# Local attention in six layers on one Trainium2 core: norms in the scores' PSUM banks, and an order of work of its own for each of four tiles

## Chip, cores and metric

One core of a Trainium2 chip runs the whole program, launched once. The metric is the time on the device in microseconds (us). The kernel before took 3695.43 us, the median of three runs (3693.75 to 3704.42).

## What is computed

For a batch of 8, 512 tokens of 128 features: a layer norm with modulation, a plain causal attention (16 heads of 8), a second modulation, and then six layers, each a windowed attention and a feed-forward. The change is in the six layers alone:

```python
def attn_layer(x, Wqkv, qs, ksc, Wo):
    q, k, v = jnp.split(x @ Wqkv, 3, -1)          # 16 heads of 64
    q, k = l2norm(q) * qs, l2norm(k) * ksc        # a norm for each token and head
    q = q * cos * scale + rotate_half(q) * sin * scale
    k = k * cos / scale + rotate_half(k) * sin / scale
    out = local_attention(q, k, v)                # windows of 32; keys of this window and the one before
    return out @ Wo
def ffn_layer(x, g, bln, W1, b1, W2, b2):
    xn = (x - mu) / jnp.sqrt(var + 1e-05) * g + bln
    a, gate = jnp.split(xn @ W1 + b1, 2, -1)
    return a * jax.nn.gelu(gate) @ W2 + b2
for i in range(6):
    x = attn_layer(shift_tokens(x), ...) + x
    x = ffn_layer(shift_tokens(x), ...) + x
```

## The kernel before

`program` calls three parts; `part_a` is the first attention, `part_c` the output, and `part_b` the six layers. `part_b` goes through NSEQ = 48 pairs of layer and batch element ("sequences"), each in TILES = 4 tiles of 128 tokens: NT = 192 tiles. All code is unrolled; each engine has its own list, written by a Python loop over steps g (`for g in STEPS`, on POOL over t), and one step does the same for every tile. What belongs to a whole sequence (output projection, mean, variance, feed-forward) is hung into the steps by `seq_at(g, lag)`, which is true in one step of four.

For a tile k the chain is: `project(c, k)` on PE multiplies x with the weights for q (c = 0) and k (c = 1), each product in three f32r passes (lines 919 to 921), into the PSUM banks `proj`. ACT squares them (`squares_of`, L1177). DVE multiplies with the two rotary tables (`turns_of`, L1385 and L1391) and sums the squares by head (`square_sums`, L1399); POOL adds the halves (`add_halves`, L1325). `norms_of` (from L1403) makes the inverse roots of the 32 sums of a tile with nine small instructions on DVE, each waiting for the one before: a clamp (L1411), a first guess from the bit pattern (L1420, with the constant table `magic`), four for a cubic step and three for a Newton step (L146 to L162). All their operands are in SBUF. In one step of four the variance of the feed-forward's norm goes along. POOL scales the heads (`scale_heads`, L1331). PE transposes (`transpose_qk(k, i)`, i = 0 to 3, L958), ACT empties into qT and kT (`qk_out`).

Scores: ACT writes the window's mask into the two PSUM banks `scr` (L1251), `score(k, half)` adds 64 matmuls of 32 queries by 64 keys on quarters of the array (L979), DVE takes the maximum (L1458) and subtracts it (L1460), ACT does exp (L1232), DVE sums and inverts (L1470, L1473), POOL scales (`L1345`). PE transposes the probabilities (`transpose_probs`, L992), and `weigh(k, half)` does 128 matmuls on quarters of the array (L1013), whose values SP has copied into place with seven DMAs per tile (L885); SP waits for the weigh of the tile before. `output` (L1028), `mean` (L1036), `variance` (L1041), `spread` (L1049), `feed_up` (L1055) and `feed_down` (L1064) follow by sequence.

PSUM is full: four banks `proj`, two `scr`, two `ring`. The ring's two banks take in turn every transpose, the values and the weighed values, ten fills a tile; `ring_order` gives the order, and PE, ACT and SP count by it.

The order of PE in one step g is: T3(g-1), score(g-1, 0), values(g-1, 0), transpose_probs(g-2, 0), score(g-1, 1), transpose_probs(g-2, 1), values(g-1, 1), project(0, g+1), weigh(g-2) in both halves, project(1, g+1), T0, T1, T2 of g, with the work by sequence in between. So score 0, score 1 and weigh are three blocks apart from one another in every step.

## Time and profile before

| | us |
|---|---|
| median of three runs | 3695.43 |
| lowest, highest | 3693.75, 3704.42 |
| profiled execution, its span | 3699.1 |
| PE busy | 3521.4 |
| DVE busy | 3039.5 |
| ACT busy | 2586.6 |
| POOL busy | 2309.1 |

TensorE's operations in the timeline from 1500 to 1565 us, from the first start to the next operation's, where nothing stalls:

| operation | us |
|---|---|
| project (6 matmuls) | 1.50 |
| values (3) | 0.79 |
| four transposes | 0.44 |
| a score half (64) | 0.79 |
| weigh, both halves (128) | 2.00 |
| feed_up (2 passes) | 0.86 |
| output (16) | 3.46 |
| feed_down (6) | 2.58 |

The six layers take from about 630 us to 3680 us. A busy PE is not PE at its peak: the ends of matmuls are modelled and overlap. "Issue" in a list of waits is idle time that no semaphore explains. PE is TensorE's matmuls, PEld its weight loads; both come from one stream of instructions.

### The profile page before, as it was taken

The page shows a single profiled execution, that of the slowest core. Times are in us where ns is not written, and L with a number is a line of the kernel's source. Part 1 is how long each engine was busy: PE and PEld are TensorE (multiplying, and loading weights), DVE is VectorE, ACT ScalarE, POOL GpSimd, SP SyncE. Part 2 cuts the span into 40 slices and gives each one's busy share as a digit, 9 for nine tenths or more (in the row PEclk, how much of TensorE's full clock was granted, in tenths as well). Part 3 has the DMA queues.
Part 4 walks back from the last instruction along what each step waited for, and adds up shares of the span by engine and source line. Part 5 has one row for each costly group of instructions (what it writes and reads, how often), then busy time and mean ns, then how long its engine had stood idle before and what let it go on. Part 6 is the DMA issues. An engine that isn't in the chain of part 4 may idle for free. (4 is left out here: it accounts for less than half of the span.)

```text
span 3699.1 us, 146879 instructions
## 1 busy us (share of the span) xinstructions
PE 3521.4 (95%) x63940; PEld 2694.0 (73%) x63940; DVE 3039.5 (82%) x4947; ACT 2586.6 (70%) x4028; POOL 2309.1 (62%) x1364
## 2 busy tenths in 40 slices
PE   6999996999999999999999999999999999999996
PEld 4777774777777777777777777777777777777774
DVE  5767766988889988888888888888898888888883
ACT  3565554677777777777777777777777777777773
POOL 1110104767777777777777767777777777776761
PEclk9999998999999999999999999999999999999998
DMA  2000001212222222222222222222222222222212
GB/s 75 4 4 7 4 7 43 56 48 58 56 58 63 64 56 58 56 56 62 58 56 58 54 56 64 56 58 55 64 63 58 56 57 54 56 56 54 54 49 68
DMA packets 121989, 188.76 MB, mean 51 GB/s; under 512 B 24942, under 2 KB 43142, under 8 KB 120972
## 3 DMA queue, kind: packets, MB, share of 16 engines
q1 hardware_dynamic: 121356, 179.36, 18.7%
q8 instruction: 514, 8.42, 1.0%
q14 instruction: 119, 0.97, 0.1%
HBM read 24.08 MB, written 4.19 MB: 8 GB/s over the span
## 5 line engine op out<-in xcount | busy, mean ns | idle before, releaser
L1325 POOL TENSOR_TENSOR rc<-rc,rs 128x1024 f32<-128x1024 f32 x384 | 912.9, 2377 | 349.2 <-DVE rs L1391 348.5
L1331 POOL TENSOR_TENSOR rc<-rc,rnorm 128x1024 f32<-128x1024 f32 x384 | 723.7, 1906 | 392.9 <-DVE rnorm L162 331.4
L1385 DVE TENSOR_TENSOR rc<-proj,rope_b 128x1024 f32<-128x1024 f32 x384 | 466.7, 1215 | 96.1 <-ACT squares L1177 89.6
L1177 ACT ACTIVATE squares<-proj 128x1024 f32<-128x1024 f32 x384 | 394.0, 1026 | 151.1 <-PE proj L921 137.6
L1013 PEld LDWEIGHTS ring<-pT,vmoved 64*64 64x64 f32 x18432 | 381.2, 135 | 132.8 <-issue 132.8
L1391 DVE TENSOR_TENSOR rs<-proj,rope_b 128x1024 f32<-128x1024 f32 x384 | 466.2, 1214 | 0.0
L958 PEld LDWEIGHTS ring<-ident,rc 128*128 128x128 f32 x3072 | 364.2, 142 | 137.5 <-issue 52.2
L1399 DVE TENSOR_REDUCE sums<-squares 128x16 f32<-128x1024 f32 x384 | 455.3, 1186 | 1.1 <-issue 0.9
L1013 PE MATMUL ring<-pT,vmoved 64*64 64x32 f32 x18432 | 407.7, 220 | 37.9 <-issue 36.4
L958 PE MATMUL ring<-ident,rc 128*128 128x128 f32 x3072 | 426.3, 277 | 11.6 <-POOL rc L1331 6.6
L1013 PE MATMUL ring<-pT,vown 64*64 64x32 f32 x6144 | 381.9, 219 | 13.8 <-issue 13.8
L1345 POOL TENSOR_TENSOR prob_b<-prob_b,rinv 128x1024 f32<-128x1024 f32 x192 | 366.4, 1909 | 12.5 <-DVE rinv L1473 12.5
L979 PEld LDWEIGHTS scr<-kT,qT 64*32 64x32 f32 x24576 | 270.3, 105 | 134.0 <-issue 133.1
L919 PE MATMUL proj<-wqkv_hi,xa_hi 128*128 128x512 f32 x768 | 344.7, 449 | 18.2 <-POOL xa_lo L1307 12.1
L979 PE MATMUL scr<-kT,qT 64*32 64x64 f32 x24576 | 338.5, 224 | 15.6 <-issue 15.2
L1028 PE MATMUL proj<-oT_b,wo 128*128 128x256 f32 x1536 | 347.6, 379 | 1.3 <-issue 1.3
L1013 PEld LDWEIGHTS ring<-pT,vown 64*64 64x64 f32 x6144 | 334.7, 135 | 12.7 <-issue 12.7
L744 DVE TENSOR_REDUCE negmax<-tm 128x1 f32<-128x384 f32 (+3 forms) x352 | 220.6, 639 | 144.5 <-PE tm L420 141.0
L586 ACT ACTIVATE probT<-km 128x512 f32<-128x512 f32 (+1 forms) x352 | 193.3, 559 | 204.9 <-PE km L436 196.6
L1168 ACT ACTIVATE kT<-ring 128x512 f32<-128x512 f32 x384 | 231.1, 602 | 139.9 <-PE ring L958 139.7
L1168 ACT ACTIVATE vown<-ring 128x512 f32<-128x512 f32 x384 | 229.0, 596 | 122.3 <-PE ring L921 111.7
L1028 PEld LDWEIGHTS proj<-oT_b,wo 128*128 128x128 f32 x1536 | 284.4, 190 | 36.2 <-issue 1.4
(176 smaller groups left out, 7886.1 us busy)
## 6 DMA issues: line engine op xcount, KB each, us to landing
vmoved<-vown SPq DMA_DIRECT2D x576, 128.0 KB
vmoved<-vown SPq DMA_DIRECT2D x192, 192.0 KB
vmoved<-vown SPq DMA_DIRECT2D x576, 64.0 KB
wqkv_raw<-in_L_ffn_Wqkv SPq DMA_DIRECT2D x40, 192.0 KB, 2.7
wo<-in_L_ffn_Wo SPq DMA_DIRECT2D x6, 512.0 KB, 4.2
x_attended<-xtok SPq DMA_DIRECT2D x8, 256.0 KB, 2.0
xtok_c<-x_attended SPq DMA_DIRECT2D x8, 256.0 KB, 4.2
out<-xtok_c SPq DMA_DIRECT2D x8, 256.0 KB, 2.4
```

Of the source, the lines that this page charges most:

```text
L958: last = nc.tensor.transpose(bank[:, p * P:(p + 1) * P], rc[:, k % 2, c, o:o + P], ident[:, :])
L979: last = nc.tensor.matmul(scr[32 * w:32 * w + 32, s, p, :], qT[rows, p, 32 * w:32 * w + 32], kT[rows, p, j * P + 32 * w:j * P + 32 * w + K ...
L1013: last[i] = nc.tensor.matmul(banks[i][64 * b:64 * b + 64, p, 32 * odd:32 * odd + 32], v[64 * s:64 * s + 64, :], pT[64 * s:64 * s + 64, p, ...
L1028: last = nc.tensor.matmul(bank[:, HALVES[half]], wo[:, p, :], oT[:, p, HALVES[half]], start=(p == 0), stop=(p == PAIRS - 1))
L1168: nc.scalar.activation(dst, src, ACT.Copy).then_inc(ring_free, 1)
L1177: nc.scalar.activation(squares[:, c, :], proj[c][:, :], ACT.Square).then_inc(sq_done, 1)
L1325: nc.gpsimd.tensor_tensor(rc[:, k % 2, c, :], rc[:, k % 2, c, :], rs[:, c, :], ALU.add).then_inc(add_done, 1)
L1331: nc.gpsimd.tensor_tensor(dst, dst, rnorm[:, k % 2, c * HEADS:(c + 1) * HEADS].rearrange("p (h o) -> p h o", o=1).broadcast_to([P, HEADS, ...
L1345: nc.gpsimd.tensor_tensor(pr, pr, rinv[:, :, :].rearrange("p q (s o) -> p q s o", o=1).broadcast_to([P, PAIRS, 2, KEYS]), ALU.mult).then_i ...
L1385: nc.vector.tensor_tensor(rc[:, k % 2, c, :].rearrange("p (h d) -> p h d", h=HEADS), proj[c][:, :].rearrange("p (h d) -> p h d", h=HEADS), ...
L1391: nc.vector.tensor_tensor(rs[:, c, :].rearrange("p (h s d) -> p h s d", h=HEADS, s=2), src[:, :, ::-1, :], tab.broadcast_to([P, HEADS, 2, ...
L1399: nc.vector.tensor_reduce(sums[:, c * HEADS:(c + 1) * HEADS], squares[:, c, :].rearrange("p (h d) -> p h d", h=HEADS), AX.X, ALU.add).then ...
```

## The change

The loops over steps go. `ring_order` and each engine's list are now written for a round of four tiles, `for n in ROUNDS`, every operation with its own tile (4n + something), in an order that differs from tile to tile. Semaphores that counted q and k together are split in two (`proj_full`, `sq_done`, `ss_done`, `turned_done`, `add_done`, `unit_done`), since q and k no longer come in a fixed turn; waits that the order gave for nothing are written out (`after`, `turned`, and some in ACT's and DVE's functions). SP's list is unchanged.

The norms use the first of the two `scr` banks (`powers`) for the sums and the running term between the subtraction of one tile's maxima and the masks of another: `norms_of(k)` waits until tile k - 2 is subtracted, and `mask_scores(k)` until the norms of tile k + 1 are done. The steps are rearranged so that no instruction has two operands in SBUF; they become ten (`cubic_powers` has five). `magic` and its memset go.

ACT and POOL now split the first chunk of the second layer's weights before their first round. In the diff, whole orders stand for PE and DVE, a stretch of ACT's; those of ACT and POOL are rewritten in the same way, with the same operations as before.

```diff
 
-LAST_STEP = NT + 6
+
+NORMS_LEAD = (1, 1, 1, 1)
+SCORES_BACK = (1, 1, 1, 1)
...
-    for g in range(-1, LAST_STEP + 1):
-        mine = [("T3", g - 1), ("V0", g - 1), ("P0", g - 2), ("P1", g - 2), ("V1", g - 1), ("O0", g - 2), ("O1", g - 2),
-                ("T0", g), ("T1", g), ("T2", g)]
+    for n in ROUNDS:
+        mine = [("T3", 4 * n + 2), ("T0", 4 * n + 2), ("T2", 4 * n + 2), ("V0", 4 * n + 2), ("P0", 4 * n + 1),
...
+def cubic_powers(nc, dve, x, y, t, w, sem, base):
+
+    ALU = mybir.AluOpType
+    dve.wait_ge(sem, base + 1)
+    nc.vector.scalar_tensor_tensor(t, x, CUBIC, y, ALU.mult, ALU.mult).then_inc(sem, 1)
+    dve.wait_ge(sem, base + 2)
+    nc.vector.tensor_tensor(t, t, y, ALU.mult).then_inc(sem, 1)
+    dve.wait_ge(sem, base + 3)
+    nc.vector.tensor_tensor(w, t, y, ALU.mult).then_inc(sem, 1)
+    dve.wait_ge(sem, base + 4)
+    nc.vector.scalar_tensor_tensor(t, t, -1.25 / CUBIC, w, ALU.add, ALU.mult).then_inc(sem, 1)
+    dve.wait_ge(sem, base + 5)
+    nc.vector.scalar_tensor_tensor(y, y, 1.875, t, ALU.mult, ALU.add).then_inc(sem, 1)
+
+
...
-        magic = sb("magic", [P, 2 * HEADS + TILES])
...
+        powers = scr[:, 0, :, :].rearrange("p q k -> p (q k)")
...
+        def norms_end(eng, k):
+            eng.wait_ge(rn_done, (min(k + NORMS_LEAD[k % TILES], NT - 1) + 1) * POWER_STEPS)
...
             def score(k, half):
...
-                pe.wait_ge(ring_free, RING[f"T{2 * half + 1}", k] + 1)
-                if half == 0:
-                    need(pe, scr_masked, k)
+                if half == 0 and k == 0:
+                    norms_end(pe, k)
+                    mask_first_scores()
+                pe.wait_ge(ring_free, max(RING[f"T{2 * half}", k], RING[f"T{2 * half + 1}", k]) + 1)
+                need(pe, scr_masked, k)
                 pe.sem_inc(pe_passed, 1)
...
+            for n in ROUNDS:
+                transpose_qk(4 * n + 2, 3)
+                project(1, 4 * n + 4)
+                after(centred, 1, n - 1, 1)
+                after(ffn_read, 1, n - 2, 1)
+                turned(0, 4 * n + 3)
+                variance(n - 1)
+                transpose_qk(4 * n + 2, 0)
+                transpose_qk(4 * n + 2, 2)
+                values(4 * n + 2, 0)
+                transpose_probs(4 * n + 1, 0)
+                after(var_read, 1, n - 1, 1)
+                after(centred, 1, n - 1, 1)
+                after(ffn_read, 1, n - 2, 1)
+                project(0, 4 * n + 4)
+                values(4 * n + 2, 1)
+                transpose_probs(4 * n + 1, 1)
+                score(4 * n + 2, 0)
+                score(4 * n + 2, 1)
+                weigh(4 * n + 1)
+                project(1, 4 * n + 5)
+                transpose_qk(4 * n + 3, 2)
+                transpose_qk(4 * n + 3, 3)
+                turned(0, 4 * n + 4)
+                spread(n - 1)
+                transpose_qk(4 * n + 3, 1)
+                turned(0, 4 * n + 4)
+                output(n, 0)
+                transpose_qk(4 * n + 3, 0)
+                values(4 * n + 3, 0)
+                after(normed, 1, n - 1, 1)
+                after(attn_added, 2, n, 1)
+                project(0, 4 * n + 5)
+                transpose_qk(4 * n + 4, 3)
+                transpose_probs(4 * n + 2, 0)
+                score(4 * n + 3, 0)
+                values(4 * n + 3, 1)
+                transpose_qk(4 * n + 4, 1)
+                score(4 * n + 3, 1)
+                transpose_qk(4 * n + 4, 0)
+                turned(0, 4 * n + 5)
+                feed_up(n - 1, 0)
+                transpose_probs(4 * n + 2, 1)
+                turned(0, 4 * n + 5)
+                feed_up(n - 1, 3)
+                weigh(4 * n + 2)
+                turned(1, 4 * n + 5)
+                feed_up(n - 1, 1)
+                turned(1, 4 * n + 5)
+                feed_up(n - 1, 4)
+                transpose_qk(4 * n + 4, 2)
+                after(gated, 3, n - 1, 1)
+                after(gelu_done, 3, n - 1, 1)
+                project(0, 4 * n + 6)
+                values(4 * n + 4, 0)
+                after(gated, 3, n - 1, 2)
+                turned(1, 4 * n + 5)
+                feed_up(n - 1, 2)
+                score(4 * n + 4, 0)
+                score(4 * n + 4, 1)
+                transpose_probs(4 * n + 3, 0)
+                transpose_probs(4 * n + 3, 1)
+                after(gelu_done, 3, n - 1, 3)
+                after(gated, 3, n - 1, 2)
+                after(gelu_done, 3, n - 1, 2)
+                project(1, 4 * n + 6)
+                weigh(4 * n + 3)
+                turned(0, 4 * n + 6)
+                feed_up(n - 1, 5)
+                values(4 * n + 4, 1)
+                transpose_qk(4 * n + 5, 0)
+                turned(0, 4 * n + 6)
+                output(n, 1)
+                transpose_qk(4 * n + 5, 1)
+                transpose_qk(4 * n + 5, 2)
+                after(attn_added, 2, n, 2)
+                after(gated, 3, n - 1, 3)
+                project(0, 4 * n + 7)
+                values(4 * n + 5, 0)
+                transpose_qk(4 * n + 5, 3)
+                project(1, 4 * n + 7)
+                values(4 * n + 5, 1)
+                transpose_probs(4 * n + 4, 0)
+                score(4 * n + 5, 0)
+                score(4 * n + 5, 1)
+                transpose_probs(4 * n + 4, 1)
+                turned(0, 4 * n + 7)
+                feed_down(n - 1)
+                weigh(4 * n + 4)
+                after(ffn_read, 1, n - 1, 1)
+                turned(0, 4 * n + 7)
+                mean(n)
+                transpose_qk(4 * n + 6, 1)
...
+            def mask_scores(k):
+                if k == 0 or not tile(k):
+                    return
+                act.wait_ge(sub_done, k)
+                norms_end(act, k)
+                mask = win_mask[k % TILES].rearrange("p (s q k) -> p s q k", s=1, q=1)
+                nc.scalar.activation(scr[:, :, :, :], mask.broadcast_to([P, 2, PAIRS, KEYS]), ACT.Copy).then_inc(scr_masked, 1)
...
+            act.wait_ge(raw_in, 16)
+            act.wait_ge(w_lo_done, BATCH)
+            split_hi(BATCH, w_raw[:, :])
...
+                exponentials(4 * n - 1)
+                gelu(n - 2, 0)
+                attention_out(4 * n - 2, 0)
+                gelu(n - 2, 1)
+                attention_out(4 * n - 2, 1)
+                qk_out(4 * n, 2)
+                mask_scores(4 * n)
+                squares_of(0, 4 * n + 2)
+                gelu(n - 2, 2)
+                values_out(4 * n, 0)
...
+            def norms_of(k):
...
+                x, t, y = powers[:, lo:hi], powers[:, 64 + lo:64 + hi], rnorm[:, k % 2, lo:hi]
                 if tile(k):
-                    dve.wait_ge(ss_done, 2 * k + 2)
-                    ss = sums[:, 0:2 * HEADS]
-                    nc.vector.scalar_tensor_tensor(ss, ss, 1e-24, ss, ALU.max, ALU.max).then_inc(clamp_done, 1)
+                    for c in range(2):
+                        dve.wait_ge(ss_done[c], k + 1)
+                        need(dve, unit_done[c], k - 1)
+                    need(dve, sub_done, k - SCORES_BACK[k % TILES])
+                    nc.vector.tensor_scalar(powers[:, 0:2 * HEADS], sums[:, :], 1e-24, None, ALU.max).then_inc(clamp_done, 1)
                 if m is not None:
                     dve.wait_ge(var_full, m + 1)
-                    nc.vector.tensor_scalar(sums[:, 2 * HEADS:], proj_bank(0, 0)[:, 0:TILES], 1e-5, None, ALU.add).then_inc(var_read, 1)
+                    need(dve, spread_done, m)
+                    if not tile(k):
+                        dve.wait_ge(sub_done, NT)
+                    nc.vector.tensor_scalar(powers[:, 2 * HEADS:hi], proj_bank(0, 0)[:, 0:TILES], 1e-5, None, ALU.add).then_inc(var_read, 1)
                     dve.wait_ge(var_read, m + 1)
                 if tile(k):
                     dve.wait_ge(clamp_done, k + 1)
-                    need(dve, unit_done, 2 * k - 2)
-                x, y, t = sums[:, lo:hi], rnorm[:, k % 2, lo:hi], rtmp[:, lo:hi]
-                nc.vector.scalar_tensor_tensor(y.bitcast(i32), x.bitcast(i32), -0.5, magic[:, lo:hi], ALU.mult, ALU.add).then_inc(rn_done, 1)
-                cubic(nc, dve, x, y, t, rn_done, i * RSQRT_STEPS)
-                newton(nc, dve, x, y, t, rn_done, i * RSQRT_STEPS)
-                dve.wait_ge(rn_done, (i + 1) * RSQRT_STEPS)
+                nc.vector.tensor_scalar(y.bitcast(i32), x.bitcast(i32), -0.5, float(0x5F3759DF), ALU.mult, ALU.add).then_inc(rn_done, 1)
+                cubic_powers(nc, dve, x, y, t, rtmp[:, lo:hi], rn_done, i * POWER_STEPS)
+                newton_powers(nc, dve, x, y, t, rn_done, i * POWER_STEPS)
...
+            for n in ROUNDS:
+                less_maxima(4 * n)
+                turns_of(1, 4 * n + 2)
+                add_attention(n - 1, 1)
+                sums_of(4 * n)
+                norms_of(4 * n + 2)
+                square_sums(0, 4 * n + 3)
+                turns_of(0, 4 * n + 3)
+                maxima(4 * n + 1)
+                less_maxima(4 * n + 1)
+                turns_of(1, 4 * n + 3)
+                sums_of(4 * n + 1)
+                centre(n - 1)
+                square_sums(1, 4 * n + 3)
+                norms_of(4 * n + 3)
+                square_sums(1, 4 * n + 4)
+                turns_of(1, 4 * n + 4)
+                turns_of(0, 4 * n + 4)
+                maxima(4 * n + 2)
+                square_sums(0, 4 * n + 4)
+                less_maxima(4 * n + 2)
+                norms_of(4 * n + 4)
+                sums_of(4 * n + 2)
+                apply_deviation(n - 1)
+                add_attention(n, 0)
+                turns_of(1, 4 * n + 5)
+                square_sums(1, 4 * n + 5)
+                turns_of(0, 4 * n + 5)
+                maxima(4 * n + 3)
+                less_maxima(4 * n + 3)
+                square_sums(0, 4 * n + 5)
+                norms_of(4 * n + 5)
+                gate(n - 1, 0)
+                gate(n - 1, 1)
+                sums_of(4 * n + 3)
+                turns_of(0, 4 * n + 6)
+                square_sums(0, 4 * n + 6)
+                maxima(4 * n + 4)
+                square_sums(1, 4 * n + 6)
+                gate(n - 1, 2)
```

## Rows read from the trace of the kernel before

**Rows 1.** The page, part 1: busy us, share of the span, instructions.
```profile
PE 3521.4 (95%) x63940; PEld 2694.0 (73%) x63940; DVE 3039.5 (82%) x4947; ACT 2586.6 (70%) x4028; POOL 2309.1 (62%) x1364
```

**Rows 2.** Busy time by window: stretch, length, busy us (instructions) per engine, granted clock, DMA.
```profile
700.00:3650.00 2950.00, 2871.74 (x58686) 2228.01 (x58684) 2551.45 (x3899) 2196.84 (x3347) 2158.23 (x1232) 1.00 0.23 57
```

**Rows 3.** Waits of PE, 700 to 3650 us: us in total, times, longest us.
```profile
PE ring L1013 <- issue: 48.5, 52, 1.8
PE scr L979 <- issue: 13.6, 30, 1.0
...
PE proj L919 <- DVE rs L1391: 1.5, 1, 1.5
```

**Rows 4.** Line 1036 (mean), its matmuls: duration ns, first and last start.
```profile
L1036 PE MATMUL proj<-xs,mean_w x96: 592/594/668, 709.7 to 3654.1; 128*128 128x512 f32 x96
```

**Rows 5.** The page, part 3: the instruction queue's packets, MB, share.
```profile
q8 instruction: 514, 8.42, 1.0%
```

**Rows 6.** Busy time by window, as rows 2, between the ends of PE's issue stalls.
```profile
1501.10:1533.31 32.21, 30.80 (x626) 24.19 (x625) 27.50 (x43) 22.80 (x36) 24.27 (x14) 1.00 0.23 58
...
1564.34:1590.88 26.54, 26.27 (x500) 20.34 (x500) 22.03 (x34) 18.89 (x31) 20.15 (x12) 1.00 0.27 69
1590.88:1596.80 5.92, 4.74 (x126) 3.86 (x125) 4.55 (x9) 3.91 (x5) 4.58 (x6) 1.00 0.01 3
```

**Rows 7.** DMA queues from 1530.5 to 1530.9 us, then PE's timeline around one stall.
```profile
q8 instruction: 1, 0.02, 17.4%
...
1531.93 0.22 PE L1013 MATMUL ring<-pT,vmoved 64*64 64x32 f32 x1
...
1533.32 0.26 PE L1013 MATMUL ring<-pT,vmoved 64*64 64x32 f32 x4 [1.18 <-issue]
```

**Rows 8.** Timeline of PE: start, us, what, merged count.
```profile
1510.68 0.60 PE L992 MATMUL ring<-ident,prob_b 128*128 128x128 f32 x4
1511.21 0.86 PE L979 MATMUL scr<-kT,qT 64*32 64x64 f32 x64
1512.00 0.66 PE L992 MATMUL ring<-ident,prob_b 128*128 128x128 f32 x4
...
1525.23 0.60 PE L992 MATMUL ring<-ident,prob_b 128*128 128x128 f32 x4
1525.66 0.95 PE L1041 MATMUL proj<-mean_w,hid 128*128 128x1 f32 x8
```

**Rows 9.** Groups of DVE, 700 to 3650 us: line, operation, count, busy, mean ns, idle before.
```profile
L1458 DVE TENSOR_REDUCE rmax<-scr 128x16 f32<-128x1024 f32 x187 | 229.0, 1224 | 25.4 <-PE scr L979 19.8
L1470 DVE TENSOR_REDUCE rsum<-prob_b 128x16 f32<-128x1024 f32 x187 | 226.0, 1208 | 2.2 <-ACT prob_b L1232 2.2
L1438 DVE SCALAR_TENSOR_TENSOR hid<-proj,vec,hid 128x512 f32<-128x512 f32 x141 | 105.7, 750 | 127.9 <-PE proj L1055 107.9 <-ACT hid L1208 20.1
L1411 DVE SCALAR_TENSOR_TENSOR sums<-sums 128x32 f32<-128x32 f32 x185 | 70.9, 383 | 3.2
L1473 DVE RECIPROCAL rinv<-rsum 128x16 f32<-128x16 f32 x187 | 47.3, 253 | 6.5
L150 DVE SCALAR_TENSOR_TENSOR rtmp<-rtmp 128x32 f32<-128x32 f32 (+1 forms) x185 | 35.7, 193 | 6.3
```

**Rows 10.** Groups of ACT and POOL, 700 to 3650 us, as rows 9.
```profile
L1168 ACT ACTIVATE oT_b<-ring 128x512 f32<-128x512 f32 x376 | 202.9, 590 | 41.8 <-PE ring L1013 41.3
L1232 ACT ACTIVATE prob_b<-prob_b 128x1024 f32<-128x1024 f32 x187 | 198.1, 1059 | 25.7 <-DVE prob_b L1460 22.8
L1208 ACT ACTIVATE hid<-proj,vec 128x512 f32<-128x512 f32 x141 | 96.5, 685 | 0.6
L1208 ACT ACT_TABLE_LOAD x47 | 60.3, 1283 | 0.8
...
L1345 POOL TENSOR_TENSOR prob_b<-prob_b,rinv 128x1024 f32<-128x1024 f32 x187 | 356.9, 1909 | 12.5 <-DVE rinv L1473 12.5
```

**Rows 11.** Timeline of SP: a tile's seven moves, issued.
```profile
1533.83 5.43 SPq L885 DMA_DIRECT2D vmoved<-vown  x7
```

628 lines of the change are left out of this document (334 added, 294 removed).

## The prediction

> **What bounds the kernel now.** I read first the page's busy shares: PE is busy for 95% of the span, DVE for 82%, ACT and POOL for less [rows 1]. Then the layers alone, by a window of 2950 us: PE 2871.74 of 2950, DVE 2551.45 (86%), at a granted clock of 1.00 [rows 2]. So TensorE sets the pace, and the question is what its remaining idle time is. The list of waits answers it: of all that PE waits for in that window, 48.5 us (52 times) and 13.6 us (30 times) are put down to "issue", which is no semaphore, and they lie in two lines, L1013 (weigh) and L979 (score). The longest wait of PE for another engine comes to 1.5 us in all [rows 3]. No engine keeps TensorE waiting: an order that only removes waits has nothing to remove here.
>
> One sequence of one layer (four tiles) I call a round. The matmuls of `mean`, one pair a round, start from 709.7 to 3654.1 us, 48 pairs [rows 4]: (3654.1 - 709.7) / 47 = 62.6 us per round, and 2950 / 62.6 = 47 rounds lie in the window.
>
> What are the issue stalls? The instruction queue q8 brought 514 packets, 8.42 MB, so 16.4 KB each [rows 5]; PE and PEld have 63940 instructions each [rows 1], and 127880 / 514 = 249 of them come with a packet. Between the end of one stall and that of another, the windows hold 626 + 625 = 1251, 500 + 500 = 1000 and 126 + 125 = 251 recorded matmuls and weight loads [rows 6]: 5, 4 and 1 times 250. Every stall thus sits on the edge of a packet. One seen closely: the packet is on the queue within 1530.5 to 1530.9, the last matmul before the gap starts at 1531.93, the next at 1533.32, some 2.5 us behind the packet [rows 7]. TensorE has run out of instructions; it had passed the rest of what it held faster than the next 16 KB came. The shown idle time starts at the modelled end of a matmul (0.22 us), so a stall is 0.2 us longer than listed: 62.1 + 82 x 0.2 = 78.5 us, over 47 rounds 1.7 us a round.
>
> Which edges stall? A weigh is 128 matmuls and 128 loads, 256 instructions in some 1.85 us (2.00 with leaving), so each holds about one edge (256 / 251). Of 47 x 4 = 188 weighs only 52 stall, 28%. The tiny matmuls are the only code that eats 16 KB in less than the 2.5 us; an edge in the first part of a weigh was ordered while longer matmuls ran. I read it so: an edge stalls if about the last 0.72 x 256 = 185 instructions before it were all of such a burst. A stall costs (48.5 + 52 x 0.2) / 52 = 1.1 us on average.
>
> **The change, part by part.** What a row-tiled block costs beside its matmuls (seams). The four transposes of L992 take 1525.66 - 1525.23 = 0.43 ahead of `variance` and 1511.21 - 1510.68 = 0.53 ahead of a score: entering costs 0.10. In a score the last of 64 matmuls starts 0.86 - 0.22 = 0.64 behind the first, and the next operation 1512.00 - 1511.21 = 0.79: leaving costs 0.15 [rows 8]. Together 0.25. Before, a tile has three such blocks (score 0, score 1, weigh), 12 a round. In the new PE order tile 4n+2 has score 0, score 1 and weigh(4n+1) in direct succession, 4n+4 and 4n+5 their two score halves together, 4n+3 all three apart: 1 + 2 + 2 + 3 = 8 blocks. Four seams go: 4 x 0.25 = 1.0 us a round, x 48 = **-48 us**. All of it is on the path, PE being dense. The matmuls themselves stay as they are, so nothing else on PE gets shorter.
>
> The supply of instructions, by the same measure. Score, score, weigh in one is a burst of 128 + 128 + 256 = 512. Edges behind its first 185: (512 - 185) / 251 = 1.3 a round. I take 1.4 us each, more than the 1.1 above, since scores pass their 128 instructions in 0.64 us, and 185 of them give the packet less cover: 1.8 us. A double score (256): (256 - 185) / 251 = 0.28 stalls of 1.6 us, 0.45, and 0.1 for edges in the few instructions right behind; two of these, 1.1. The other three weighs 0.28 x 1.1 = 0.3 each, 0.9. The single score halves of tile 4n+3 as now, 0.1 (13.6 + 6 = 20 us / 188 tiles). Together 3.9 us a round against 1.7: +2.2, x 48 = **+106 us**. Bounds: from nothing (the burst is fed after all) to 1.3 x 2.0 (the longest seen, 1.8 + 0.2 [rows 3]) + 2 x 0.7 + 1.0 = 5.0, that is +3.3, +158 us. I take 2.2 because it uses the mean share that stalls now.
>
> Waits. Before there are next to none on PE. In the new order several chains end near where TensorE needs them; the tightest that I find is from score(4n+3) to transpose_probs(4n+3, 0), worked out under the rivals, with 0.6 us left before any hand-off. A few such places, and stalls that shift one engine against another, I take at 0.4 us a round, **+19 us**; bounds 0 and 2 us a round (0 and +96). A wait of PE gives a packet time to land, and both won't be paid where they meet: -10 us.
>
> The norms. Nine small instructions per tile become ten. Most take 193 ns, the first 383 [rows 9]. No row has DVE write PSUM; the nearest small ones are 193 ns and, with 16 columns and another operation, 253 [rows 9]: ten of them are 1.9 to 2.5 us against about 2.0 now, between -0.1 and +0.5 us a tile. DVE has 14% idle, 8.5 us a round; covered, nothing. What it costs is an order: the operands lie in `scr`, so norms(k+1) stands between less_maxima(k-1) and mask_scores(k), on which score(k) waits. That loop (less_maxima, norms, masks as long as an exp, two score halves, maxima, and a turn of DVE besides) is 1.22 + 2.2 + 1.0 + 1.6 + 1.22 + 1.22 = 8.5 us of some 15.7 per tile, and it doesn't set the pace by itself. The memset of `magic` on POOL goes, before anything is measured by it.
>
> At the start ACT now waits for the first chunk of the next layer's weights before its first round (a transfer and a split, before there was anything to hide it): **+4 us**, once; the tail keeps its chain. The DMAs and their bytes stay. SP's seven moves of a tile's values still wait for the weigh of the tile before, and the next weigh for them: issuing them takes 5.43 us [rows 11], landing the last about 1 more. The shortest way in the new order is from weigh(4n+2) to weigh(4n+3), with two feed_up, transposes, project, values, feed_up, two scores, two transposes and project between; by the table of TensorE's operations ahead of the prediction (seams off where halves join) 0.86 x 2 + 0.44 + 1.5 + 0.8 + 0.86 + 1.4 + 0.87 + 1.5 = 9.1 us. 2.6 us are left; covered, nothing.
>
> Sum: -48 + 106 + 19 - 10 + 4 = +71 us. The profiled execution has a span of 3699.1, 3.7 over the median of 3695.4 and inside the spread of the runs; put on the median, 3695.4 + 71 = **3766 us**.
>
> **The rivals.** (a) The supply doesn't get worse, and the seams are saved: -48 + 4 + 0 to 19, 3651 to 3670 us, faster. For it: the share of edges that stall is inferred, not seen, and none of the bursts before is longer than 256. A lead that grows in the slow parts might carry over. Against it: a weigh alone uses up what is held, in 28 of 100 cases. The Trainium skill (Runtime: NRT & Kernel Launch, Instruction fetch mechanics) says that instructions are refilled in blocks of 16 KiB, 256 instructions, and that crossing such a block is mostly hidden, since dispatch is slower than the refill; by that rule this rival is right. The block agrees with the trace (16.4 KB, 251 recorded), the hiding doesn't: 82 stalls in 47 rounds.
>
> (b) The waits decide, on the other side: the chain for the probabilities of tile 4n+3. From the end of its scores DVE does maxima and less_maxima, 2 x 1.22; ACT exp (1.06), a table load of 1.28, gelu 0, one `attention_out` and gelu 1 (0.69 + 0.59 + 0.69), which DVE's gate 1 (0.75) needs, and behind that gate stand sums_of (1.21 + 0.25) and POOL's scale_probs (1.91): 2.4 + 4.3 + 0.75 + 1.46 + 1.91 = 10.9 us, counted from 0 [rows 9, 10]. TensorE has in that stretch T0, feed_up 0, P1, feed_up 3, weigh, feed_up 1 and 4, T2, project, values, feed_up 2 and two scores: 0.44 + 0.86 + 0.44 + 0.86 + 2.0 + 1.7 + 0.44 + 1.5 + 0.8 + 0.9 + 1.6 = 11.5 us by the same table. 0.6 us are left; some eight hand-offs eat it. From there each us is a us a round. Two such places one us late each, beside the supply stalls: +96, 3862 us.
>
> (c) Supply and seams cancel (+1.0 a round instead of +2.2): within 10 us of 3695. This is also what comes out if the new order does nothing for PE, which was never waiting.
>
> **How the numbers follow.** Forecast, 0.55: 3766, its own range 3715 to 3815. (a) 0.20, (b) 0.15, (c) 0.10. Beyond 0.3% (11 us), about what a measurement of this kernel tells from no change: faster 0.22 ((a) and 0.02 of (c)), same 0.10 (0.06 of (c), 0.04 at the lower edge of the forecast), slower 0.68 (0.51, (b), and 0.02 of (c)). The range for 8 in 10 reaches into (a) and (b): 3650 to 3860.
>
> **What would show it.** Right: the round between two `mean` 63.5 to 64.5 us; PE's waits for "issue" about twice as long, most in the weigh behind the two score halves, at multiples of 250 instructions; blocks entered 8 times a round; POOL's and DVE's waits no shorter. Seams: PE busy time per round falls by about 1 us. Wrong: issue stalls at 1.7 us a round or less and a round near 61.5 (rival a); or waits of PE's transposes of the probabilities for POOL, of its scores for ACT's masks, over 1 us a round (rival b). The prediction falls if the stalls don't grow with the length of a burst.

## The result, and the profile after

The changed kernel takes 3876.75 us (median; 3873.32 to 3878.99), the kernel before 3694.65 beside it (3693.75 to 3704.42): a ratio of 1.0496, 95% interval 1.0476 to 1.0516. It is 182 us slower. The prediction, 3766 us, had the direction but only 71 of these 182 us, and the time lies 17 us above its range. Every run's time is the median of executions within 1% of each other; one execution of e7 further down, at 8090.3 us where its other three took 3778.11 to 3795.49, is unexplained and left out.

The page after (parts 1 to 3), to be held against [rows 1, 5]:

```profile
span 3877.1 us, 150543 instructions
...
PE 3569.4 (92%) x63940; PEld 2740.4 (71%) x63940; DVE 3017.2 (78%) x5140; ACT 2590.9 (67%) x4028; POOL 2302.6 (59%) x1363
...
PEclk9999997999999999999999999999999999999997
...
q8 instruction: 517, 8.47, 0.9%
```

The code has grown by three packets only, and PE has the same 63940 matmuls. They take 48 us more of busy time, though the order spares seams: part of them ran at a lower clock. Its mean over the span is 0.966 against 0.987 before. Busy time by window, the layers and then the stretches between the ends of three stalls (against [rows 2, 6]):

```profile
700.00:3650.00 2950.00, 2766.96 (x55585) 2156.88 (x55584) 2420.22 (x3898) 2092.72 (x3183) 2055.31 (x1181) 0.97 0.20 54
...
1729.61:1733.34 3.73, 2.07 (x129) 1.87 (x128) 3.70 (x4) 0.00 (x0) 3.27 (x3) 1.00 0.02 4
1733.34:1766.92 33.58, 31.26 (x623) 24.43 (x623) 24.44 (x42) 23.20 (x35) 21.23 (x12) 0.95 0.20 52
```

257 and 1246 recorded instructions, one and five packets: stalls sit on the edges of packets as before. But the mean granted clock is 0.97 where it was 1.00. The matmuls of `mean` (line 1089 now) give the round, the four tiles of one sequence, (3831.1 - 718.4) / 47 = 66.2 us against 62.6 [rows 4]:

```profile
L1089 PE MATMUL proj<-xs,mean_w x96: 590/645/1220, 718.4 to 3831.1; 128*128 128x512 f32 x96
```

Their median is 645 ns and the longest 1220; before these were 594 and 668 [rows 4]. A matmul of 1220 ns ran at half the clock. Waits of PE from 700 to 3750 us (us in total, times, longest), 46 rounds, against [rows 3]. The lists of waits of the experiments run from 700 to 3700 us, so they hold some 46 rounds of the faster kernels and 41 of the slowest:

```profile
PE ring L1066 <- issue: 98.1, 75, 2.4
PE scr L1030 <- issue: 51.1, 40, 2.0
PE ring L960 <- ACT qT L1248: 18.5, 46, 0.4
PE ring L1044 <- ACT vown L1248: 6.8, 14, 1.3
```

**Where 182 us went.** The table divides the round of each kernel. All rows are taken from the first `mean` to the last, 47 rounds. Supply: all waits of PE for "issue" plus 0.2 us for each of them (as the prediction counted), by 47. Other waits: those of PE for ACT, DVE, POOL, counted likewise. Low clock: the time in which the trace grants 1.2 instead of 2.4 GHz, halved, since half of it is lost to an engine that is busy (an upper figure where PE idles in it: over the time in which PE is busy alone it is 1.71 after and 0.22 before). Rest: what remains, PE's own work with its seams, a seam being what PE pays to enter and to leave a block of tiny matmuls. Each row is one profiled execution.

| kernel | round | supply | other waits | low clock | rest |
|---|---|---|---|---|---|
| before | 62.65 | 1.84 | 0.20 | 0.22 | 60.39 |
| after | 66.23 | 3.78 | 1.11 | 1.84 | 59.50 |
| after, long burst apart (e1) | 65.20 | 2.48 | 2.09 | 0.92 | 59.71 |
| e1, score halves apart too (e2) | 64.81 | 1.73 | 2.17 | 0.76 | 60.15 |
| e2, `project` in halves (e6) | 64.63 | 1.96 | 1.61 | 0.71 | 60.35 |
| e6, `project` earlier (e7) | 64.19 | 2.12 | 0.95 | 0.75 | 60.37 |
| after, norms in SBUF (e4) | 72.24 | 3.49 | 5.67 | 3.79 | 59.29 |
| before, scores ahead of weigh (e3) | 73.01 | 6.34 | 4.52 | 2.69 | 59.46 |
| before, scores together (e10) | 64.83 | 2.87 | 1.65 | 0.76 | 59.55 |
| before, a wait ahead of weigh (e8) | 70.07 | 1.66 | 5.24 | 4.03 | 59.14 |
| before, weigh around project 1 (e5) | 65.50 | 0.37 | 4.13 | 0.00 | 61.00 |
| before, weigh and project interleaved (e9) | 63.21 | 0.73 | 0.21 | 0.04 | 62.23 |

From before to after, over 47 rounds: supply 1.94 x 47 = +91 us, low clock 1.62 x 47 = +76 (+70 by PE's busy time), other waits 0.91 x 47 = +43, rest -0.89 x 47 = -42. That is +168; the start is 8.7 us longer (first `mean` at 718.4 against 709.7) and the tail 1.1: the 178 us between the spans.

**The clock behind a stall.** PE's timeline of the changed kernel, a stall inside a weigh and the output projection that follows it, and the windows before, behind and well behind:

```profile
1766.92 0.19 PE L1066 MATMUL ring<-pT,vmoved 64*64 64x32 f32 x1 [1.55 <-issue]
...
1770.55 4.22 PE L1081 MATMUL proj<-oT_b,wo 128*128 128x256 f32 x16
```

```profile
1763.66:1768.00 4.34, 2.79 (x131) 2.30 (x130) 1.22 (x1) 1.45 (x2) 1.57 (x1) 1.00 0.02 4
1768.30:1771.70 3.40, 3.40 (x11) 2.83 (x11) 3.00 (x4) 1.78 (x4) 0.00 (x0) 0.51 0.02 5
1772.00:1776.00 4.00, 4.00 (x24) 3.53 (x23) 2.03 (x3) 2.51 (x4) 0.00 (x0) 1.00 0.71 187
```

In the middle window the granted clock is 0.51, so 1.2 GHz; PE is busy for all of its 3.40 us and gets through 11 matmuls. The output projection takes 4.22 us; the same 16 matmuls of the kernel before, at the full clock:

```profile
1503.38 3.62 PE L1028 MATMUL proj<-oT_b,wo 128*128 128x256 f32 x16
```

This stall thus costs twice: 1.6 us at once, and about as much again behind it. On average it is less, since not each stall lowers the clock: 1.84 us a round for 3.78 us of stalls. From 700 to 3650 us the clock falls 36 times in the changed kernel (25 times for 3.4 us, 10 for 6.8, once for 10.2) and 6 times before (3.4 us each). Each time, here and in all the experiments, PE had been idle for 1.2 us or more within the 2.6 us ahead. Idles of PE in that stretch (shown time plus 0.2 us), and how many are followed by a fall within some 2.5 us:

| idle, us | before | after | e7 | e5 | e8 |
|---|---|---|---|---|---|
| 0.8 to 1.2 | 28, 0 | 19, 0 | 16, 0 | 185, 0 | 15, 0 |
| 1.2 to 1.6 | 26, 4 | 26, 8 | 19, 0 | 1, 0 | 23, 2 |
| 1.6 to 2.0 | 6, 2 | 51, 28 | 16, 5 | 1, 0 | 1, 0 |
| 2.0 to 2.7 | none | 11, 5 | 10, 10 | none | none |
| 5.2 | none | none | none | none | 42, 42 |

Executions of one kernel differ in the same way: of seven of the kernel before, the fastest (3688.85 us) had a mean clock of 0.989, the slowest (3709.32) one of 0.985.

### The profile page after: what moved, and what is told of

Read it like the earlier page. It is cut to its first block and busy times, and to the rows that moved or that the text cites. A ratio compares the mean times of both kernels' runs of the same rounds, so it can differ in the third digit from the quotient of the medians.

```text
span 3877.1 us, 150543 instructions
## 1 busy us (share of the span) xinstructions
PE 3569.4 (92%) x63940; PEld 2740.4 (71%) x63940; DVE 3017.2 (78%) x5140; ACT 2590.9 (67%) x4028; POOL 2302.6 (59%) x1363
## 5 line engine op out<-in xcount | busy, mean ns | idle before, releaser
L1594 DVE TENSOR_REDUCE sums<-squares 128x16 f32<-128x1024 f32 x384 | 465.6, 1212 | 84.1 <-ACT squares L1259 74.4
L1066 PEld LDWEIGHTS ring<-pT,vmoved 64*64 64x64 f32 x18432 | 397.9, 137 | 176.8 <-issue 172.2
L1066 PE MATMUL ring<-pT,vmoved 64*64 64x32 f32 x18432 | 425.4, 222 | 78.9 <-issue 71.5
L1005 PEld LDWEIGHTS ring<-ident,rc 128*128 128x128 f32 x3072 | 378.8, 147 | 123.8 <-issue 68.8
L1005 PE MATMUL ring<-ident,rc 128*128 128x128 f32 x3072 | 453.6, 282 | 10.5 <-POOL rc L1506 6.0
L1248 ACT ACTIVATE oT_b<-ring 128x512 f32<-128x512 f32 x384 | 214.2, 595 | 320.3 <-PE ring L1066 320.3
L1066 PE MATMUL ring<-pT,vown 64*64 64x32 f32 x6144 | 399.0, 222 | 28.7 <-issue 28.6
L1066 PEld LDWEIGHTS ring<-pT,vown 64*64 64x64 f32 x6144 | 355.1, 138 | 29.2 <-issue 29.1
L1030 PE MATMUL scr<-kT,qT 64*32 64x64 f32 x24576 | 311.8, 225 | 51.3 <-issue 51.1
L962 PE MATMUL proj<-wqkv_hi,xa_lo 128*128 128x512 f32 x768 | 315.6, 411 | 0.0
```

What stands on the lines that cost most here:

```text
L1005: last = nc.tensor.transpose(bank[:, p * P:(p + 1) * P], rc[:, k % 2, c, o:o + P], ident[:, :])
L1030: last = nc.tensor.matmul(scr[32 * w:32 * w + 32, s, p, :], qT[rows, p, 32 * w:32 * w + 32], kT[rows, p, j * P + 32 * w:j * P + 32 * w + K ...
L1066: last[i] = nc.tensor.matmul(banks[i][64 * b:64 * b + 64, p, 32 * odd:32 * odd + 32], v[64 * s:64 * s + 64, :], pT[64 * s:64 * s + 64, p, ...
L1248: nc.scalar.activation(dst, src, ACT.Copy).then_inc(ring_free, 1)
L1594: nc.vector.tensor_reduce(sums[:, c * HEADS:(c + 1) * HEADS], squares[:, c, :].rearrange("p (h d) -> p h d", h=HEADS), AX.X, ALU.add).then ...
```

## The experiments

The first four ran on one chip beside the kernel before (3701.13 us there), the next four beside 3697.31, the last two beside 3691.72. My theory at first was the prediction's: bursts of tiny matmuls outrun the supply, and what the supply doesn't explain is waits; the rivals were that waits alone make the time, and for the norms that their new place costs or saves. The clock joined the theory before the first four ran. None of the ten times fell into the range of the theory that it was to bear out; those of e4, e6 and e7 fell into a rival's.

**e1: the long burst taken apart in the new order.** From the changed kernel:

```diff
-                values(4 * n + 2, 1)
-                transpose_probs(4 * n + 1, 1)
                 score(4 * n + 2, 0)
+                values(4 * n + 2, 1)
                 score(4 * n + 2, 1)
-                weigh(4 * n + 1)
+                transpose_probs(4 * n + 1, 1)
                 project(1, 4 * n + 5)
+                weigh(4 * n + 1)
```

> The changed kernel with one edit in PE's order: the burst of score 0, score 1 and weigh in tile 4n+2 is parted (score 0, values, score 1, transposes, project, weigh); the other engines' lists stay. Theory S (supply and clock): that burst holds 2.1 us of the 3.6 us of supply stalls a round and most of the low clock behind them. It goes to about 0.3 us, -85 us over 47 rounds; the time at the low clock (171 us in the layers, of which half is lost) falls to some 80 us, -45; two seams come back, +24. Some 3770 us (3750 to 3800). Theory W (the waits of the new order are the cost, the supply only fills them): the waits stay and the seams come back, 3870 to 3900 us.

Measured: 3825.36 us, ratio 1.0341 (1.0315 to 1.0368), 51 us faster than the changed kernel (expected: 3770 by S, 3870 or more by W; it came out between them). Waits of PE:

```profile
PE ring L1066 <- issue: 54.5, 45, 2.0
PE scr L1030 <- issue: 40.3, 40, 2.0
PE ring L1005 <- ACT oT_b L1248: 37.1, 46, 1.1
```

The weigh's stalls go from 75 to 45 and from 98 to 54.5 us, while the score's stay. Supply falls by 1.30 us a round (61 us) and the low clock with it by 0.92 (43 us). The gain isn't the whole 104 us: a new wait came, PE's T2 for ACT's emptying of the weighed values, 46 times, once a round. The edit itself makes it, since the `project` that stood between that weigh and T2 now stands ahead of the weigh.

**e2: all score halves apart as well.** From e1:

```diff
                 score(4 * n + 4, 0)
-                score(4 * n + 4, 1)
                 transpose_probs(4 * n + 3, 0)
+                score(4 * n + 4, 1)
                 transpose_probs(4 * n + 3, 1)
...
                 score(4 * n + 5, 0)
-                score(4 * n + 5, 1)
                 transpose_probs(4 * n + 4, 1)
+                score(4 * n + 5, 1)
```

> As the kernel before this one, and the two score halves of tiles 4n+4 and 4n+5 parted too, each by a transposition of probabilities: 12 blocks a round again, as in the kernel before. S: stalls of the double scores (35 us) fall to about 8, the clock gives 20 back, two seams cost 24: some 3750 us (3730 to 3780), and what is left over the kernel before is waits, 40 to 60 us. W: 3890 us or more.

Measured: 3811.53 us, ratio 1.0304 (1.0276 to 1.0333).

```profile
PE ring L1066 <- issue: 45.2, 36, 1.9
PE ring L1005 <- ACT oT_b L1248: 37.3, 46, 1.1
PE scr L1030 <- issue: 20.7, 30, 1.5
PE ring L960 <- ACT qT L1248: 18.6, 46, 0.6
```

Supply is where it was before the change (1.73 us a round; before 1.84), so the length of the bursts is what had doubled it. But the time stays 110 us above the kernel before. 2.0 us a round of it are waits for other engines, 0.5 the clock. I had put e2 at 3750. Of the waits 1.0 us a round is the one that e1's edit made; the rest, about 1.0, belongs to the new order.

**e6: half of that `project` behind the weigh**, so that T2 comes later. From e2 (`project` takes a part, its waits and its signal go with the first and the last half):

```diff
-                project(1, 4 * n + 5)
+                project(1, 4 * n + 5, (0,))
                 weigh(4 * n + 1)
+                project(1, 4 * n + 5, (1,))
```

> The kernel with all bursts parted (3811 us), with project 1 of tile 4n+5 split: three of its six matmuls go ahead of weigh(4n+1), three behind, so that both the emptying of the transposes before it and that of its own banks have cover. Theory R (the rest over the kernel before is waits of the new order at a few fixed places): the wait of L1005 for the emptied weighed values, 37.3 us in 46 rounds and 0.2 more each than shown, goes: -45, and a few us of the clock: 3755 to 3775. Rival R2 (another wait takes its place, since ACT is what is late in that stretch): above 3795.

Measured: 3808.32 us, ratio 1.031 (1.028 to 1.034): no gain, as the rival R2 had it (R: 3755 to 3775).

```profile
PE ring L1068 <- issue: 51.5, 37, 2.3
...
PE ring L1068 <- ACT pT L1251: 10.3, 46, 0.5
```

The wait of T2 for `oT_b` is gone (46 times 0.8 us), but only 0.18 us of it is won in each round: the weigh now waits for ACT's `pT`, and PE's rest and supply are 0.2 us longer each. Here the wait that was removed came back at other places.

**e7: `project(0, 4n + 4)` ahead of the values and the transposes.** From e6:

```diff
-                values(4 * n + 2, 0)
-                transpose_probs(4 * n + 1, 0)
                 after(var_read, 1, n - 1, 1)
                 after(centred, 1, n - 1, 1)
                 after(ffn_read, 1, n - 2, 1)
                 project(0, 4 * n + 4)
+                values(4 * n + 2, 0)
+                transpose_probs(4 * n + 1, 0)
```

> As the kernel before this one, and project 0 of tile 4n+4 moved ahead of values 0 of 4n+2, which waits once a round for a bank that ACT empties late (18.6 us in 46, about 28 with the hidden part). R: -25, 3730 to 3750. R2: no gain, as the masks on ACT follow and the scores now come sooner behind them: 3765 or more, with a wait of the scores for ACT.

Measured: 3778.11 us, the median of three, ratio by their mean 1.0232 (1.02 to 1.0264).

```profile
PE ring L1068 <- issue: 48.7, 33, 2.4
PE scr L1032 <- issue: 29.0, 34, 1.6
PE ring L1068 <- ACT pT L1251: 11.6, 46, 1.1
```

The time lies in R2's range (3765 or more), but R2's wait of the scores for ACT doesn't show; R's 3730 to 3750 was set from e6's expected time, which had missed. The step was forecast at -25 us and gave -30 by the medians, -21 by the rounds (64.63 to 64.19 us, x 47): other waits fall from 1.61 to 0.95. With that the whole time is still 81 us above the kernel before: supply 0.28 us a round, other waits 0.75, clock 0.53, start and the rest nothing of weight. Note the clock: supply is nearly that of before, but there it came in many short stalls (48.5 us in 52 and 13.6 in 30 [rows 3], 0.93 and 0.45 us each), here in fewer long ones at the weigh (48.7 us in 33, 1.48 us each; 0.85 at the scores). The 15 falls of its clock all stand behind long ones, one behind each of the ten idles above 2.0 us.

**e3: the long burst put into the kernel before**, in each of the four tiles (the two score halves moved from between values and transposes):

```diff
+                if tile(g - 1):
+                    score(g - 1, 0)
+                    score(g - 1, 1)
                 if tile(g - 2):
                     weigh(g - 2, 0)
```

> The kernel before with one edit in PE's order: in every step both score halves are moved behind project 0, straight in front of weigh, so that each tile has one burst of 512 instructions; nothing else changes. S: supply stalls from 78 us to 4 x 2.1 = 8.4 us a round, some 390 us, +310; clock +150; eight seams a round fewer, -94: some 4060 us (3950 to 4150), with stalls at multiples of 250 recorded instructions. W (the length of a burst doesn't matter): the seams saved, and the scores 2.5 us later on DVE's list: 3600 to 3720 us.

Measured: 4194.12 us, ratio 1.1331 (1.1296 to 1.1366).

```profile
PE ring L1013 <- issue: 216.0, 155, 2.2
PE ring L992 <- ACT vown L1168: 50.9, 122, 0.7
PE ring L919 <- ACT qT L1168: 38.1, 122, 0.8
```

The theory of the supply said 4060 (3950 to 4150), that of the waits alone 3600 to 3720. The stalls of the weigh go from 52 in 47 rounds to 155 in 41. Supply costs 4.5 us a round more, that is 1.1 per burst of 512 instructions (the prediction had 1.8 for one, less the 0.3 of the weigh in it: 1.5). My expectation was 134 us too low, and its parts were further off than that: over 47 rounds supply is +212 us (+310 expected), the clock +116 (+150), and other waits, for which it had nothing, are +203, most of them of PE for ACT, since the scores now come later in the step. e3 thus shows what the joined burst does to the stalls; its time is not that of the supply alone.

**e10: only the score halves together in the kernel before**, 256 instructions, in the place of the second:

```diff
-                    score(g - 1, 0)
                     values(g - 1, 0)
...
                 if tile(g - 1):
+                    score(g - 1, 0)
                     score(g - 1, 1)
```

> The kernel before with the two score halves of a tile in succession, in the place of the second, and weigh apart as it was: bursts of 256 instructions in 1.3 us. The sizes in question: four seams a round fewer, -47; supply stalls of double scores, 4 x (256 - 177) / 256 x 1.6 us = 2.0 a round against 0.4 for the parted halves, +75; the clock behind them +25. About 3745 us (3720 to 3770). If a seam were worth more than the stalls: below 3695.

Measured: 3789.8 us, ratio 1.026 (1.024 to 1.0279), 20 us above the expected range.

```profile
PE scr L979 <- issue: 55.5, 37, 2.1
PE ring L1013 <- issue: 43.8, 51, 1.6
PE ring L919 <- ACT qT L1168: 42.3, 137, 0.4
```

Of the extra 2.18 us a round supply is 1.03, the clock 0.54, waits 1.45, and the rest falls by 0.84: the four seams that it saves, forecast at 1.0. The expectation had no term for the waits, 68 us over 47 rounds. Joining two scores doesn't pay even by itself. A double score stalls 37 times in 188 for 1.5 + 0.2 us each, 20 in 100; the prediction had 28 in 100 at 1.6. The timeline gives the seam directly: where nothing stalls, a double score lasts 1.44 us to the next operation (median of 87) and a half 0.79, so 0.14 us of leaving is saved, and 0.10 of entering [rows 8].

**e8: a wait in the kernel before**, in one of four steps, with nothing moved:

```diff
                 if tile(g - 2):
+                    if j == 2 and tile(g - 1):
+                        pe.wait_ge(inv_done, g)
                     weigh(g - 2, 0)
```

> The kernel before, with one more wait of PE: in one step of four, ahead of weigh, it waits until DVE has inverted the sums of the tile just scored. No instruction is moved, the bursts stay as they are. Theory C (any idle time of PE over some 1.2 us lowers the granted clock for 3.4 to 6.8 us, whatever it waits for): some 2 us more a round, +95, and in a quarter to a half of the rounds a lowered clock, +20 to +40: 3810 to 3840 us, with the time at the low clock from 20 to 60 or 100 us in the layers. Rival (only a lack of instructions lowers it): the clock stays as before, 3790 us or less.

Measured: 4062.24 us, ratio 1.099 (1.0966 to 1.1014). Waits of PE, and the layers by window:

```profile
PE ring L1013 <- DVE rinv L1475: 215.3, 43, 5.0
PE ring L1013 <- issue: 37.7, 46, 1.4
```

```profile
700.00:3650.00 2950.00, 2685.71 (x52576) 2098.79 (x52558) 2301.87 (x3517) 1974.48 (x3010) 1948.88 (x1120) 0.94 0.20 52
```

The wait came out at 5 us and not at the 2 I had meant, so the expected time is no test. What it shows is that the clock also falls behind an idle that is no lack of instructions: with fewer and shorter "issue" stalls than before (37.7 against 48.5 us) the time at 1.2 GHz goes from 20 to 379 us, and each of the 42 waits of 5 us from 700 to 3650 us is followed by a fall. The wait itself is 5.0 us a round, the round longer by 7.4. Nothing was moved, so the other 2.4 us are the clock's, by elimination; the table's 3.81 more is too high here, since PE is idle in 76 of the 379 us. By its busy time it is 3.0.

**e5: the kernel before with `project(1, g+1)` between the halves of weigh**, so that no burst is longer than 128 instructions (the expectation calls it project 0; what stands between is `project` of c = 1, all six matmuls):

```diff
                     weigh(g - 2, 0)
-                    weigh(g - 2, 1)
                 if tile(g + 1):
...
                     project(1, g + 1)
+                if tile(g - 2):
+                    weigh(g - 2, 1)
                 if tile(g):
                     transpose_qk(g, 0)
```

> The kernel before with weigh in two halves of 128 instructions and the second half of project 0 between them; nothing else moved. Supply theory: no weigh has 185 instructions in one any more, its stalls (57 us) go, those of the scores (20) stay, and nothing is left that lowers the clock; a seam more in each tile is 0.25 to 0.35 us, +47 to +66: 3685 to 3710 us against 3695. If the stalls came from something else at that place (a bank, a port), they stay: 3740 to 3760.

Measured: 3837.55 us, ratio 1.0375 (1.0355 to 1.0395), far above both expected ranges.

```profile
PE ring L958 <- ACT oT_b L1169: 145.7, 181, 0.8
PE scr L979 <- issue: 10.0, 17, 1.5
...
PE ring L1013 <- issue: 0.2, 1, 0.2
```

The stalls of the weigh vanish (52 to 1), so they do come from the length of the burst, and no time is left at 1.2 GHz between the first `mean` and the last. In their place T0 waits 0.8 us for ACT's emptying of the second half, in nearly every tile.

**e9: halves of weigh and of `project(1, g+1)` in turn**, which gives T0 its distance back:

```diff
                     weigh(g - 2, 0)
-                    weigh(g - 2, 1)
...
-                    project(1, g + 1)
+                    project(1, g + 1, (0,))
+                if tile(g - 2):
+                    weigh(g - 2, 1)
+                if tile(g + 1):
+                    project(1, g + 1, (1,))
```

> The kernel before with weigh in two halves and the first half of project 1 (not of project 0, whose squares ACT has ahead of the weighed values) between them. Supply theory: stalls fall as in the kernel that split around project 0, to 0.4 us a round (-62), the low clock goes (-10), a seam more per tile is +47 to +56; if ACT now empties the weighed values in time, 3680 to 3710 us; if the 0.75 us of matmuls behind weigh, instead of 1.5, are too short for that, up to 0.3 us a tile more, 3765 at most.

Measured: 3724.6 us, ratio 1.0094 (1.0078 to 1.0111), 15 us above the expected range of 3680 to 3710.

```profile
PE scr L980 <- issue: 12.5, 26, 1.5
PE ring L1014 <- issue: 5.7, 17, 0.6
```

and one parted weigh, with the half of `project` between:

```profile
1504.48 0.22 PE L1014 MATMUL ring<-pT,vown 64*64 64x32 f32 x1
1504.62 0.50 PE L919 MATMUL proj<-wqkv_hi,xa_hi 128*128 128x512 f32 x1
1504.96 0.39 PE L920 MATMUL proj<-wqkv_lo,xa_hi 128*128 128x512 f32 x1
1505.18 0.40 PE L921 MATMUL proj<-wqkv_hi,xa_lo 128*128 128x512 f32 x1
1505.51 0.32 PE L1014 MATMUL ring<-pT,vmoved 64*64 64x32 f32 x8
```

Supply 1.11 us a round less, clock 0.18 less, no new wait, and yet slower: the rest grows by 1.84, and it has four seams more. That would be 0.46 us each, but the lines show less: 0.14 us from the last matmul of the weigh to the next operation where one follows another in 0.02, 0.34 for the first pass of `project` where one takes 0.22, and 0.33 from its last pass to the weigh. That is some 0.33 us for a seam with `project` behind it, 1.3 of the 1.84, against 0.25 at the scores [rows 8], and the rest grows by only 0.61 in e5, which has the same four seams. What the other 0.5 of e9 is stays open. No kernel here beats the one before: where supply and clock were won, seams or waits took more.

**e4: the norms back in SBUF in the new order**, with nine instructions, nothing else changed:

```diff
-                x, t, y = powers[:, lo:hi], powers[:, 64 + lo:64 + hi], rnorm[:, k % 2, lo:hi]
+                x, t, y = sums[:, lo:hi], rtmp[:, lo:hi], rnorm[:, k % 2, lo:hi]
...
-                    need(dve, sub_done, k - SCORES_BACK[k % TILES])
...
-                cubic_powers(nc, dve, x, y, t, rtmp[:, lo:hi], rn_done, i * POWER_STEPS)
-                newton_powers(nc, dve, x, y, t, rn_done, i * POWER_STEPS)
+                cubic(nc, dve, x, y, t, rn_done, i * RSQRT_STEPS)
+                newton(nc, dve, x, y, t, rn_done, i * RSQRT_STEPS)
```

> The changed kernel with its order, and the norms as before: operands in SBUF, nine instructions instead of ten, no wait of the norms for the subtraction and of the masks for the norms. S: DVE isn't the bound, so within 12 us of 3877. W: if the loop through the scores' banks is among the waits that cost, 3877 - 40 or less; if the SBUF operands hold DVE up where the new order lets POOL work at the same time, 3877 + 20 or more.

Measured: 4171.01 us, ratio 1.1282 (1.1239 to 1.1324): a clear miss of S, which expected no difference from the changed kernel; the second half of W, DVE held up beside POOL, had the direction. Groups of DVE from 700 to 3700 us (mean ns behind the comma), first of e4:

```profile
L156 DVE TENSOR_TENSOR rtmp<-rnorm 128x32 f32<-128x32 f32 (+1 forms) x165 | 201.7, 1222 | 5.6
L1622 DVE SCALAR_TENSOR_TENSOR rnorm<-sums,magic 128x32 int32<-128x32 int32 (+1 forms) x165 | 196.2, 1189 | 6.2 <-DVE sums L1612 0.4 <-DVE sums L1618 0.3
```

then of the changed kernel:

```profile
L179 DVE SCALAR_TENSOR_TENSOR scr<-scr,rnorm 128x32 f32<-128x32 f32 (+1 forms) x181 | 36.2, 200 | 6.2
L1622 DVE TENSOR_SCALAR rnorm<-scr 128x32 int32<-128x32 int32 (+1 forms) x181 | 34.8, 192 | 6.2
```

Thirty-two columns take 1.2 us on average with all operands in SBUF, and 0.2 with one in PSUM. The timeline of e4, POOL beside DVE:

```profile
1511.81 1.91 POOL L1514 TENSOR_TENSOR prob_b<-prob_b,rinv 128x1024 f32<-128x1024 f32 x1 [7.21 <-DVE rinv L1650]
1511.89 1.87 DVE L1622 SCALAR_TENSOR_TENSOR rnorm<-sums,magic 128x32 int32<-128x32 int32 x1
...
1513.67 2.40 POOL L1493 TENSOR_TENSOR rc<-rc,rs 128x1024 f32<-128x1024 f32 x1
...
1513.80 2.32 DVE L156 TENSOR_TENSOR rtmp<-rnorm 128x32 f32<-128x32 f32 x1
```

POOL's instruction ends at 1513.72 and DVE's at 1513.76; the next pair at 16.07 and 16.12. This is the rule in e4, from 700 to 3650 us: of 241 norm instructions of 32 columns with two operands in SBUF that start while one of POOL's runs, 232 end within 0.1 us of it, and those that start alone take 192 ns. In the changed kernel the norms start beside POOL more than 1100 times and take 187 to 199 ns on average all the same. The Trainium skill (SBUF — State Buffer, section "SBUF: two separate sides") has the reason, that the two engines share a pair of ports under an exclusive lock, which a DVE operation with two SBUF inputs needs against a POOL operation that reads SBUF; the ends above agree. What it does to PE:

```profile
PE proj L1126 <- DVE rs L1585: 111.8, 40, 3.3
```

Other waits are 5.67 us a round instead of 1.11, and with long idles come 3.79 of low clock. In the kernel before the same instructions in SBUF take 193 ns, and 383 for the first [rows 9], because there they run while POOL waits for them, but for the first, which starts beside POOL in 131 of 185 cases: in one step seen closely they start at 1510.65, POOL's last instruction ends at 1509.46 and its next, which needs their result, starts at 1512.73. Norms in PSUM are thus what makes the new order bearable, worth 4171 - 3877 = 294 us in it. In the old one there seems to be next to nothing to gain, by these rows; no run has the norms in PSUM in the old order.

## Why the prediction was right in direction and too low by 111 us

**The bound.** Right. TensorE sets the pace, and nothing before was waiting for another engine. An order that joins and parts operations on PE had only seams to win.

**Supply, +106 us forecast, +91 measured.** Right in mechanism and place, and in the sum: 3.78 us a round where 3.9 was written. e3 and e2 show cause and cure: with the burst joined in the old order the stalls triple, with the bursts apart in the new one they are back at 1.7. The share of edges was inferred from one number (28%), and held roughly: of the 62 stalls within the bursts of 512 instructions the earliest lie at the 145th and the 177th, where I had written 185. That the sum is so close is partly luck, for the terms were off both ways. In the changed kernel the burst of 512 costs 2.15 us (1.8 forecast; 1.5 each in e3), the two double scores 0.78 (1.1), the three other weighs 0.72 (0.9), the single score halves nothing (0.1).

**The step that failed, a term that wasn't there: the clock, +70 to +76 us.** The prediction priced a stall at its idle time alone and put what comes behind it at nothing, without a reason. This is the largest part of the error of 111 us, and it could have been seen. [Rows 2] have a mean of 1.00, and I took that as a constant. The mean of the whole span was 0.987, and the trace of before holds some 6 falls in the layers, each behind an idle of over 1.2 us. A stall of 1.0 us, as before, mostly leaves the clock alone; of the 62 in the new burst, 1.63 us on average, 28 are followed by a fall. So the price of a stall isn't in proportion to its length. e3 (253 us at 1.2 GHz), e4 (356) and e8 (379) show it for supply, for waits for DVE through a slow DVE, and for a bare wait; e5 and e9, in which the long stalls are gone, have 0 and 3.

**Seams, -48 forecast, -42 measured** by the column "rest" (-0.89 us a round for four blocks fewer), and -0.84 in e10 for four. Right at the scores, as the length of e10's double scores confirms. The column takes up whatever the clock term has too much, so it is no exact measure. A seam with `project` behind it costs more, some 0.33 by e9's timeline.

**Waits, +19 forecast, +43 measured**, within the bounds (0 to +96). The places are ACT's emptying of a bank of q for the values (46 times 0.4 us) and of the values for the transposes. Whether the discount of 10 us for overlap was right no run shows: the waits do grow to 2.1 with the bursts apart (e1, e2), but by the one new wait that e1's edit makes, not by waits that stalls had hidden.

**Norms: covered, nothing.** DVE's ten instructions take 187 to 200 ns each, at the lower end of the estimate, so writing PSUM costs nothing extra. The verdict holds for the change as made. What I had not seen is that the move and the order hang together: I priced each alone, and e4 shows 294 us between them.

**Start +4, measured +9; tail +1.** What the 9 us are isn't shown: the same start gives +5 to +11 in e1, e2, e6 and e7. SP's moves: no wait of weigh for them shows, as forecast. With the clock +76, the waits 24 above their term, the discount 10, the seams 6, start and tail 6, and the supply 15 under, the terms account for 107 of the 111 us.

**The rivals.** (a), the supply doesn't grow, is refuted by the trace after and by e3. The Trainium skill's sentence (Runtime: NRT & Kernel Launch, Instruction fetch mechanics) that crossing a block is mostly hidden doesn't hold in these bursts: 121 stalls in 47 rounds, up to 2.4 us each. (b) named a chain for the probabilities of tile 4n+3 through POOL at 3862 us. Its time was the nearest, by luck, for its mechanism isn't in the trace: between the first and the last `mean` PE waits for POOL's `prob_b` once, for 2.2 us, and for ACT's masks never. POOL itself waits 514 us in all for DVE's inverses (12.5 before [rows 10]), and that costs PE nothing. (c), that supply and seams cancel, fell with the supply.

**The range** ended at 3860 because it held the worst of each known term and none for what a longer stall does to the clock. My marks for "right" (a round of 63.5 to 64.5, "issue" twice as long, stalls at multiples of 250) came in for the stalls and not for the round, and the difference between the two, 66.2 against 64.5, is the clock for the most part, with the waits above their term. PE's busy time per round, which was to fall by 1 us, grows (3569.4 against 3521.4 us in all): the low clock hides the seams in it.

**What stays open.** Why of two idles of equal length one lowers the clock and the other doesn't. How the 43 us of other waits would divide if no stall lay among them; e1 and e2 carry a wait of their own and don't tell. And the rest of e3, which is 0.93 us under that of before where eight seams fewer should give 2.0.

## What to carry to other kernels

Where TensorE is the bound and has bursts of tiny matmuls, count instructions per burst before joining blocks: a joined block saves a seam (0.25 us here), and one edge of the instruction queue far enough inside it costs 1.6 us and, on average in the changed kernel, half as much again in clock (1.84 for 3.78 us a round). Price an idle of a dense TensorE by its length: around 1 us it costs itself (none of e5's 185 was followed by a fall), from 1.2 us on look at the granted clock behind it. And when an engine's list is rewritten, look which engine runs beside each small DVE instruction with both operands in SBUF; there the same code can take six times as long.
